# Placing of tiles in a mixture-of-experts layer: rank and row base read from PSUM without a copy

## The reference

```python
x: [32, 256, 256, 1]        # images
h = wavelet_tokens(x)       # three Haar levels, each band weighted by a gate, and back
h = concat([cls_tok, h])    # 32 x 257 rows of 256
h = h + attention(layernorm(h), R)              # causal, one head
h = h + ffn(layernorm(h), ...)

def ffn(x, gate_w, gamma, beta, fc1s, b1s, fc2s, b2s):
    xf = x.reshape(-1, 256)                     # 8224 rows
    k, n = 8224 // 8, 8                         # 1028 rows for each of 8 experts
    scores = (tanh(xf @ gate_w.T) + 1) * 0.5
    vals, idx = top_k(scores.T, k)              # each expert picks its k best rows
    y = layernorm(xf[idx], gamma, beta)
    h = gelu(y @ fc1s.T + b1s)                  # 256 -> 1024
    o = (h @ fc2s.T + b2s) * vals               # 1024 -> 256
    return xf.at[idx].add(o)
```

## Time and profile before

| | us |
|---|---|
| median of 3 runs | 826.06 (826.01 to 826.22) |
| the profiled execution | 825.02 |
| its span, first to last instruction | 823.2 |

### The profile page before, as it was taken

One profiled execution on the slowest core, in us unless ns is written; L12 is line 12 of the kernel. 1 busy time (PEld: TensorE's weight loads), 2 busy tenths in 40 slices (PEclk: granted clock), 3 DMA queues, 4 the chain that ended last, 5 costly groups with the idle time before them and its releaser, 6 DMA issues.

```text
span 823.2 us, 15855 instructions
## 1 busy us (share of the span) xinstructions
PE 722.4 (88%) x4684; PEld 652.6 (79%) x4684; DVE 575.7 (70%) x1902; ACT 441.4 (54%) x971; POOL 462.3 (56%) x680
## 2 busy tenths in 40 slices
PE   6988999999999974845799999999889999999994
PEld 3976777777777763734698999998889999899994
DVE  3674899999999967998776684666736746744441
ACT  1002677777777774102565566656545666556551
POOL 0155587777877754206158557485564674855533
PEclk9989999999999995555999999999979999999997
DMA  9800022122221127301125335243343342433222
GB/s 295 259 1 1 30 77 78 55 73 76 76 76 60 69 81 146 102 0 53 58 41 129 64 65 132 40 107 83 55 123 49 71 124 41 111 77 53 40 26 27
DMA packets 63579, 64.35 MB, mean 78 GB/s; under 512 B 14032, under 2 KB 57104, under 8 KB 63376
## 3 DMA queue, kind: packets, MB, share of 16 engines
q1 hardware_dynamic: 50576, 46.32, 18.1%
q0 software_dynamic: 12800, 17.12, 13.0%
q10 hardware_dynamic: 128, 0.00, 0.0%
HBM read 37.90 MB, written 25.53 MB: 77 GB/s over the span
## 4 chain that ended last, share of the span: by engine, by line
PE 33%; issue 9%; DVE 8%; POOL 6%; ACT 3%; DMA 2%; POOLq 0%; ACTq 0%; DVEq 0%; SPq 0%
PE bank L973 15%; PE bank L987 13%; POOL w2l L515 2%; PE bank L999 2%; POOL out L551 2%; POOL yg L529 2%; DMA raw<-in_fc1T 2%; PE bank L962 2%; ACT bank L713 1%; DVE Tc L1400 1%; DVE yl L1519 1%; PE bank L952 1%; DVE TR L1384 1%; DMA yg<-rows,idx 1%; DVE jk L1496 1%
## 5 line engine op out<-in xcount | busy, mean ns | idle before, releaser
L551 POOL DMA_INDIRECT out<-ob,sidx x72 | 113.9, 1583 | 161.4 <-ACT ob L729 149.7
L1526 DVE TENSOR_TENSOR hl<-bank,hh 128x384 fp32r<-128x384 f32 (+1 forms) x192 | 97.6, 513 | 144.6 <-ACT hh L716 141.2
L713 ACT ACTIVATE bank<-bank,b1s 128x384 f32<-128x384 f32 (+1 forms) x192 | 99.5, 518 | 146.8 <-PE bank L973 142.4
L973 PE MATMUL bank<-yh,w1h 128*128 128x384 f32 (+1 forms) x384 | 133.2, 347 | 10.6 <-DVE hl L1526 3.8
L973 PE MATMUL bank<-yl,w1h 128*128 128x384 f32 (+1 forms) x384 | 123.5, 322 | 2.0 <-issue 2.0
L973 PE MATMUL bank<-yh,w1l 128*128 128x384 f32 (+1 forms) x384 | 124.1, 323 | 0.0
L987 PE MATMUL bank<-w2l,hh 128*128 128x256 f32 x384 | 108.0, 281 | 0.0
L987 PE MATMUL bank<-w2h,hh 128*128 128x256 f32 x384 | 108.0, 281 | 0.0
L987 PE MATMUL bank<-w2h,hl 128*128 128x256 f32 x384 | 107.9, 281 | 0.0
L529 POOL DMA_INDIRECT yg<-rows,idx x72 | 72.4, 1006 | 56.6 <-issue 51.5
L716 ACT ACTIVATE hh<-bank 128x384 fp32r<-128x384 f32 (+1 forms) x192 | 87.7, 457 | 6.1
(11 more groups left out here) (225 smaller groups left out, 1801.1 us busy)
## 6 DMA issues: line engine op xcount, KB each, us to landing
BIG<-in_x SPq DMA_DIRECT2D x4, 2048.0 KB, 14.4
out<-Bs SPq DMA_DIRECT2D x32, 256.0 KB, 2.1
rows<-Yp SPq DMA_DIRECT2D x32, 256.0 KB, 2.3
raw<-in_fc1T SPq DMA_DIRECT2D x16, 512.0 KB
raw<-in_fc2T SPq DMA_DIRECT2D x16, 512.0 KB
yg<-rows,idx POOLq DMA_INDIRECT x72, 2.9
out<-ob,sidx POOLq DMA_INDIRECT x72, 3.8
gwb<-in_gate_w SPq DMA_DIRECT2D x1, 1024.0 KB, 7.2
```

What stands on the lines that cost most here:

```text
L551: g.indirect_dma_start(out=out_rows, out_offset=tok(ap=sidx[job.eh][0:m, t:t + 1], axis=0), in_=ob[t % 3][0:m, :], in_offset=None, compute ...
L713: A.activation(h[:, 0:cur.w], h[:, 0:cur.w], ACT.Gelu_apprx_tanh, bias=b1s[:, bass.ds(cur.e, 1), f]).then_inc(s["hact"], 1)
L973: last = T.matmul(Lb[ring(cur, f)][:, 0:cur.w], w1s[cur.eh][i][:, d, f * P:(f + 1) * P], yT[cur.p][k][:, d, 0:cur.w], start=(n == 0), stop ...
L1526: v.tensor_tensor(hT[cur.p][1][:, f, 0:cur.w], Lb[ring(cur, f)][:, 0:cur.w], hT[cur.p][0][:, f, 0:cur.w], ALU.subtract).then_inc(s["hlo"], 1)
```

## The change

The copy into `SM` goes, and `SM` with it. The rank takes its two pointer scalars straight from PSUM, and `rowf` takes its input from there. `rowf` moves from behind the count to ahead of it, and both signal once, together: the semaphore `row` counts one for each tile instead of three, and the wait ahead of the index is for `smc` alone. The placing matmul, its release by `smc`, and everything else stay.

```diff
-        SM = sb("SM", [P, 9, 3])
...
-                r0 = n * 3
                 B = place_bank(job, t)
                 dve.wait_ge(s["smm"], n + 1)
-                v.tensor_copy(SM[0:m, t, :], B[0:m, NT:NT + 3]).then_inc(s["row"], 1)
-                dve.wait_ge(s["row"], r0 + 1)
-
-                v.tensor_scalar(rk[0:m, t:t + 1], cst("slot")[0:m, t:t + 1], SM[0:m, t, 1:2], SM[0:m, t, 2:3],
-                                ALU.subtract, ALU.subtract).then_inc(s["row"], 1)
-                dve.wait_ge(s["row"], r0 + 2)
-
+                v.tensor_scalar(rk[0:m, t:t + 1], cst("slot")[0:m, t:t + 1], B[0:m, NT + 1:NT + 2], B[0:m, NT + 2:NT + 3],
+                                ALU.subtract, ALU.subtract)
+                v.tensor_scalar(rowf[0:m, t:t + 1], B[0:m, NT:NT + 1], float(NT), -1.0, ALU.mult, ALU.add)\
+                    .then_inc(s["row"], 1)
+                dve.wait_ge(s["row"], n + 1)
                 v.tensor_scalar(jk[0:m, :], B[0:m, 0:NT], rk[0:m, t:t + 1], None, ALU.is_le, ALU.add,
                                 accum_out=pos[0:m, t:t + 1]).then_inc(s["smc"], 1)
-                v.tensor_scalar(rowf[0:m, t:t + 1], SM[0:m, t, 0:1], float(NT), -1.0, ALU.mult, ALU.add)\
-                    .then_inc(s["row"], 1)
                 dve.wait_ge(s["smc"], n + 1)
-                dve.wait_ge(s["row"], r0 + 3)
                 v.tensor_scalar(idx[job.eh][0:m, t:t + 1], pos[0:m, t:t + 1], rowf[0:m, t:t + 1], None, ALU.add)\
                     .then_inc(s["ixd"], 1)
```

## The result

The changed kernel takes 822.44 us (median of 22 executions, 818.58 to 825.35); the kernel before, measured anew beside it, 825.13 (22 executions, 822.91 to 828.44). The ratio is 0.9967, with a 95% interval of 0.9955 to 0.9979: faster by 0.33%. Over the runs of this study together the kernel before has a mean of 825.7 us (157 executions, all but the 22 above) and the changed one 822.7 (51 executions), 3.0 us less. The forecast was 1.2 us, so the direction was right, and the size was short by more than half.

The account below looks back on a forecast made before the run. TensorE, busy 88% of the span, was taken as the bound, with placing gains only between 367 and 402 us at once. Terms 0.45 + 0.48 + 0.26 = 1.19 us took 826.06 to 824.9 us, range 823.4 to 826.9.

Parts of the forecast that it names:

- C: In each tile on VectorE, the count starts 0.12 us sooner, 0.38 instead of 0.50 after the tile's start.
- F: A whole tile on VectorE is 0.26 us shorter, 1.04 instead of 1.30.
- The rivals of PSUM pointers: Rank's pointers cost more from PSUM: double leaves 0.35 us gain (chance 0.15); dear makes it slower (chance 0.07).
- a change that does not do what it says: Rival: first gather not released by its index, or first job bound by ScalarE; little or nothing, 826.0; chance 0.05.
- Up to the first real matmul: The start, from first tile through gathers, scaling and `yl`: 0.26 + 0.19 = 0.45 us sooner.
- GpSimd's own pace of 1.55 us: At the start, later gathers follow the first at this pace, so they move by 0.26 us only.
- the 0.19 for tile 6: Ahead of `yl` at the start, tile 6 gives another 0.26 us, of which only 0.19 can be used.
- four C and one F: First job's five counts on the chain of waits, 387.98 to 430.28: four give 0.48 us, the one at 398.23 gives 0.26.
- After 437 us I count nothing: The other tiles lie beside full matmul queues and gathers run an expert ahead, so they give no time.
- my own sign of being wrong: TensorE waits after 437 us differing by over 0.3 us, rank over 0.45 us, or an unmoved first gather would refute it.
- The port: At experts' ends `ohu`, coming 0.52 us sooner, gets ahead of `w2l`; at 706 alone, gain 2.02 us; chance 0.15.
- The clock: At the loop's turn, 594 to 600 us, earlier work shifts the clock's return: 823.5 or 826.3; chance 0.13.

Follow-up runs that it names:

- the first 27 alone: New form of placing in the 27 tiles of the first three experts, old form in the other 45, against the kernel before: 0.9984, repeated 0.9982.
- the later 45 alone: Old form of placing in the first 27 tiles, new form in the 45 of the five later experts, against the kernel before: 0.9979, repeated 0.9988.

## Why the prediction was right or wrong

**The tile** was right in each term: 0.27 for the rank, C = 0.12, F = 0.26, 1.04 a tile. The rivals of PSUM pointers are out. So is that of a change that does not do what it says, as the first gather did follow its index.

**Up to the first real matmul** I had 0.45 and the profiles show 0.6. The first mask was ready 0.19 us later in the changed kernel's profile, by no doing of the change (its matmuls start at 367.82 against 367.64); with that taken off, scaling comes 0.40 sooner, where I had 0.26. The short step is "GpSimd's own pace of 1.55 us" for the gathers, which was a wait for the index: the third gather started 1.61 us behind its index (372.02) in the kernel before, and 1.61 behind it in the run with the copy kept, at a pace of 1.40. In the changed kernel it starts at 373.27, 1.84 behind its index and 1.26 behind the second gather. ScalarE's rounding moves with the scaling by 0.40, and `yl` by 0.60, so the 0.19 for tile 6 held.

**The first three experts' tiles in all**: 1.19 forecast, 1.2 measured in time, 1.6 in span, 0.9 at equal clock. From the first real matmul to the second expert's first (381.62 to 436.36 in the kernel before) six profiles with the old form take 54.7 to 56.8 us, nine with the new 54.7 to 56.0, in the mean 0.8 less (standard error 0.3), where my four C and one F make 0.74. So these terms are borne out, but no closer than some 0.3 us: that 1.19 met 1.2 so exactly is luck.

**"After 437 us I count nothing. The eight experts' other tiles lie beside full matmul queues"** is the step that failed. It put the term for 45 of the 72 tiles at nothing, and the runs show 1.5 us (standard error 0.26) in its place, 1.0 at equal clock. I read the nothing from TensorE's waits, and they hardly say otherwise: from the second expert's first matmul to the last transposes TensorE idles for 15.8 to 16.2 us in four profiles with the old form in the later tiles and for 14.2 to 16.8 in six with the new. The same stretch takes 374.0 to 375.0 us with the old and 372.3 to 374.3 with the new, 0.9 less in the mean. Half of that is in the fourth expert, whose end is the loop's turn, no more exactly than that. By my own sign of being wrong, waits after 437 us that differ by more than 0.3 us, the `hl` and `oT` rows would have told, at 0.8 us each; but they cancel, and four profiles of the changed kernel differ by up to 1.5 in the sum. Why the shorter tiles are worth 1.5 us, that is, what in TensorE's time answers to them, stays open.

**The port**, as I named the rival in which `ohu` gets ahead of `w2l`, did not turn. Why `ohu` waits no run shows, only that it does, to 0.56 us past the end of `w2l`. At three of the six ends `ohu` moved up by 0.42 to 0.49 us, where I had 0.52; at the other three by 0.71 to 0.78, nearer to three F than to the two that I had. So all six are ties, starts within 0.10 us, and not three. Each went to GpSimd. At two ends the records even have `ohu` starting first, by 0.10 and 0.03 us, and it waited all the same. What I had called a lost 0.52 us was lost, and the sum was not meant to have it.

**The clock** I had as a rival at one place, the turn, for the moment at which the work arrives there (granted clock 0.50 of the full rate in the earlier trace rows). What the runs show is a difference in how often the clock is low: 57 of 157 executions of the kernel before have a mean granted clock of 0.933 or less, and 1 of 51 of the changed one. In time at half rate, reckoned as above, that is 107.8 us against 104.0. At the fit's 0.25 us for each, 3.8 x 0.25 = 0.9 us of the 3.0 go with the clock, and 2.1 are left at equal clock. The single profiles don't contradict this price: with the turn at half rate for 10.2 us the kernel before takes 111.5 us from the fourth expert's first second-layer matmul to the sixth's, and with 6.8 us 110.5. Why low executions are rarer is open, and so is whether it is the later tiles' doing: the first 27 alone have 3 such executions of 24, the later 45 alone 2 of 24, and the kernels with a part of the later tiles in the new form 5 and 8 of 12.

So the account is 1.2 us for the tiles that I had costed, and 1.5 for those I had left out, with some 0.9 of the two going with the clock by the fit; the 0.3 to the whole's 3.0 is within the uncertainty.

## What to carry to other kernels

An engine's time beside a busy TensorE is not free because no wait names it. Where a loop of four engines is nearly balanced, take work away or put some in at that place alone, and time it: here some 12 us of VectorE taken away gave 1.5 us, and 8.5 put in cost 0.9 (clear of noise only at equal clock), with the waits view unchanged. Keep the dose small: four times as much made waits of its own and measured those. Small PSUM operands were best read in place here: a copy to SBUF ahead of them bought nothing. And where an instruction of one engine waited for one of another, `ohu` for `w2l`, moving it up to the other's start gained nothing (it still ended 0.56 us behind `w2l`) until it was out of the other's way altogether (0.74 us long instead of up to 3.08), and then the next wait was already there: of 4.6 us of waits removed 1.1 came back as time.

## What the runs showed of the hardware

- The rank, a VectorE instruction with one column per partition and two pointer scalars, takes 275 ns in the mean of 64 with the pointers in PSUM and 273 with them in SBUF; `rowf`, with one column and no pointer, takes 147 ns with its tensor in PSUM and 149 with it in SBUF.
- `ohu` waits for GpSimd's `w2l` when the two start together. With recorded starts up to 0.10 us apart, VectorE's ahead in some of them, `w2l` took its 2.35 to 2.42 us in all cases of the changed kernel, and `ohu` ended 0.56 to 0.57 us behind it. So a recorded start does not decide a tie. The first end of the changed kernel:

```profile
437.94 3.08 DVE L1470 TENSOR_SCALAR ohu<-iot,begM 128x1028 bf16<-128x1028 f32 x1
438.04 2.42 POOL L514 TENSOR_TENSOR w2l<-raw,w2h 128x1024 fp32r<-128x1024 f32 x1
```
- `oh`, a VectorE instruction with two tensor inputs in SBUF, waits for GpSimd's subtraction as well where it starts beside it: it ends 1.10 us behind it at all six ends (1.29 us long where it runs behind the subtraction, 1.98 to 2.29 here). The scatter behind that subtraction takes longer too (2.38 us instead of 1.85; 1.58 in the mean of 72).
- The form of `ohu` that also sums takes 1.26 to 1.28 us beside the subtraction and 1.26 alone, so it does not wait for it; the plain form takes 0.73 alone and up to 3.08 beside it.
- Executions of one kernel scatter over 5 to 7 us, and the mean granted clock orders them in part: for the changed kernel a mean of 821.9 us of span at 0.934, 821.4 at 0.936, 820.3 at 0.938 (13, 17 and 11 executions).
